# GpSimd adds both halves of a state step to the running sum with one instruction

## What is computed

```python
A_disc = jnp.exp(-jnp.exp(A_log)[None, None] * dt[..., None])
Bx = Bp[:, :, None, :] * dt[..., None] * xs[..., None]
C = Cp @ W_C.T
def step(s, inp):
    A_t, Bx_t = inp
    s = A_t * s + Bx_t
    return (s, s.sum(-1))
...
y = C * ssum + D_param * xs
```

## Time and profile before

| | |
|---|---|
| three runs | 1182.11, 1183.95, 1184.22 us |
| median | 1183.95 us |
| span of the profiled execution | 1183.4 us |
| mean granted TensorE clock | 0.925 of full speed |
| instructions | 15564 |
| HBM traffic | 139.46 MB read, 26.77 MB written |

### The profile page before, as it was taken

The page is one execution under the profiler, slowest core; times in us unless marked ns, Lnnn a source line. Parts: engine busy times, 40 slices in busy tenths (PEclk is TensorE's granted clock), DMA queues, the critical chain, the costliest instruction groups (busy, mean ns, idle before and its releaser), DMA issues.

```text
span 1183.4 us, 15564 instructions
## 1 busy us (share of the span) xinstructions
PE 1028.6 (87%) x4732; PEld 828.0 (70%) x4732; DVE 657.2 (56%) x1148; ACT 642.2 (54%) x1240; POOL 671.5 (57%) x658
## 2 busy tenths in 40 slices
PE   7676497877977878988969899799999999999997
PEld 4323275655656556766757788689999999998886
DVE  7898999899997889877975332001000000110233
ACT  5776778787586786885672433133333333333342
POOL 0755867768589987789695447422433333322221
PEclk9798598888987888999989999899999999999999
DMA  6710100202002016142374582688999988863521
GB/s 195 258 36 1 49 23 19 71 1 89 2 18 72 1 50 218 37 133 80 99 214 141 157 258 59 169 281 245 349 345 310 307 272 275 268 183 63 169 72 54
DMA packets 142244, 166.84 MB, mean 141 GB/s; under 512 B 26424, under 2 KB 127056, under 8 KB 142016
## 3 DMA queue, kind: packets, MB, share of 16 engines
q1 hardware_dynamic: 126480, 147.12, 38.2%
q0 software_dynamic: 15680, 18.72, 8.3%
HBM read 139.46 MB, written 26.77 MB: 140 GB/s over the span
## 4 chain that ended last, share of the span: by engine, by line
PE 45%; POOL 22%; issue 13%; DVE 9%; ACT 6%; SPq 2%; DMA 1%; DVEq 0%; POOLq 0%; ACTq 0%
PE psum L1243 19%; POOL Ssum L1929 10%; PE psum L1210 9%; PE psum L1222 6%; PE psum L1199 6%; POOL list_d L1948 4%; DVE S L1470 3%; ACT A L1771 2%; POOL acc_d L1979 1%; DVE psum L1431 1%; PE psum L1165 1%; POOL gb L1937 1%; POOL scale L1850 1%; PE psum L1186 1%; DMA bb<-b 1%
## 5 line engine op out<-in xcount | busy, mean ns | idle before, releaser
L1929 POOL TENSOR_TENSOR Ssum<-Ssum,S 128x512 f32<-128x512 f32 x217 | 274.3, 1288 | 71.0 <-DVE S L1470 69.9
L1243 PE MATMUL psum<-w,hT 128*128 128x256 f32 x1136 | 255.4, 383 | 7.0 <-issue 5.6
L1243 PEld LDWEIGHTS psum<-w,hT 128*128 128x128 f32 x1136 | 215.7, 192 | 37.5 <-issue 6.7
L1979 POOL DMA_INDIRECT acc_d<-y,ID x71 | 112.8, 1589 | 223.1 <-DMA acc_d<-y,ID 116.5
L1210 PE MATMUL psum<-XT,w 128*128 128x256 f32 x800 | 184.8, 388 | 15.3 <-DMA bb<-b 7.5
L1771 ACT ACTIVATE A<-dts,nea 128x512 f32<-128x512 f32 x245 | 167.6, 717 | 33.9 <-DVE S L1470 27.9
L1210 PEld LDWEIGHTS psum<-XT,w 128*128 128x128 f32 x800 | 153.7, 194 | 43.0 <-issue 12.9
L1431 DVE TENSOR_TENSOR psum<-us,psum 128x512 f32<-128x512 f32 x234 | 149.3, 683 | 34.8 <-PE psum L1116 34.4
L1470 DVE TENSOR_TENSOR_SCAN S<-A,carry,psum 128x512 f32<-128x512 f32 x120 | 148.2, 1264 | 0.0
L1815 ACT ACTIVATE hT<-psum,bb 128x256 f32<-128x256 f32 x200 | 83.4, 472 | 94.9 <-PE psum L1210 94.7
L1595 DVE COPY XT<-psum 128x512 f32<-128x512 f32 x35 | 24.2, 691 | 192.9 <-PE psum L1186 192.8
(11 more groups left out here) (185 smaller groups left out, 1263.9 us busy)
## 6 DMA issues: line engine op xcount, KB each, us to landing
w<-W SPq DMA_DIRECT2D x92, 1024.0 KB, 7.3
bb<-b SPq DMA_DIRECT2D x46, 128.0 KB, 8.1
xnb<-x SPq DMA_DIRECT2D x16, 256.0 KB, 3.0
Xr<-x SPq DMA_DIRECT2D x16, 256.0 KB, 4.4
x_d<-gb SPq DMA_DIRECT2D x8, 512.0 KB, 2.9
xn_d<-nb SPq DMA_DIRECT2D x8, 512.0 KB, 3.1
X<-x_d SPq DMA_DIRECT2D x16, 256.0 KB, 8.7
ACC<-acc_d SPq DMA_DIRECT2D x16, 256.0 KB, 6.3
```

Of the source, the lines that this page charges most:

```text
L1243: t = eng.matmul(bank(g)[:, 256 * k:256 * k + 256], hT[n % 2][:, f, 128 * k:128 * k + 128], w[:, f, :], start=f == 0, stop=f == 7)
L1929: eng.tensor_tensor(to, to, of, ALU.add).then_inc(nsum, 1)
L1979: eng.indirect_dma_start(acc_d, bass.IndirectOffsetOnAxis(ap=ID[:, col, 1:2].bitcast(u32), axis=0), y[n % NY][:, k, :], None, compute_op=A ...
```

## The change

The two tiles of a running sum become one of 128 x 2 x 512, and `S0[i][c]` are views of it. In chunks 1 to 7 GpSimd adds nothing at even k; at odd k one instruction adds two neighbouring slots to both halves. It raises `nsum` by 2. The wait for the scan stays at every k. In chunk 0 nothing changes.

```diff
-        S0 = [[put(f"Ssum{i}{c}", [128, 512]) for c in range(2)] for i in range(2)]
+        Ssum = [put(f"Ssum{i}", [128, 2, 512]) for i in range(2)]
+        S0 = [[Ssum[i][:, c, :] for c in range(2)] for i in range(2)]
...
-                    if n and (i or c and n < EARLY):
-                        to, of = S0[i % 2][c], S[:, s % NS, :]
-                        if i % 2 == 0 and n == 1:
-                            eng.wait_ge(carried, CARRIES * (i // 2) + c + 1)
+                    if i == 0 and c and 0 < n < EARLY:
+                        to, of = S0[0][1], S[:, s % NS, :]
+                        if n == 1:
+                            eng.wait_ge(carried, 2)
                         if n > 1:
                             eng.wait_ge(nsum, added_by_pool(i, k - 2))
                         eng.tensor_tensor(to, to, of, ALU.add).then_inc(nsum, 1)
+                    elif i and c and n:
+                        to, of = Ssum[i % 2], S[:, s % NS - 1:s % NS + 1, :]
+                        if i % 2 == 0 and n == 1:
+                            eng.wait_ge(carried, CARRIES * (i // 2) + 2)
+                        if n > 1:
+                            eng.wait_ge(nsum, added_by_pool(i, k - 2))
+                        eng.tensor_tensor(to, to, of, ALU.add).then_inc(nsum, 2)
```

## The result

| | before | after |
|---|---|---|
| median, 21 runs each | 1182.24 us | 1185.31 us |
| lowest to highest | 1181.14 to 1184.22 | 1182.37 to 1189.68 |
| span of the profiled execution | 1183.4 us | 1181.6 us |

The ratio is 1.0025, 95% interval 1.0018 to 1.0032: the change costs 3.1 us by the medians. In a later measurement, where the kernel before had a median of 1188.01 us, the ratio was 1.0034 (1.0021 to 1.0047). The direction and the range hold; the size was forecast at +5.4 us, and 3.1 came. The spans of the two profiled executions point the other way. The reason is the stretch of transfers and routing between about 700 and 790 us, which differs between executions of one kernel: two traces of the kernel before are together at 710 us, 14.5 us apart at 727 and 3.3 us apart from 784 on.

A forecast was written before the change was run, and what follows sets the result against it. No engine bounds the whole; in the scan stage the path runs through GpSimd's adds and `scale`. Losses of +2.8 and +2.6 us gave +5.4 on 1183.95, so 1189.3 us; 8-in-10 range 1182 to 1193.

The forecast's parts named there:

- The start: The median of three runs of the kernel before, 1183.95 us, to which the forecast adds +5.4 us.
- The duration of a pair: One GpSimd add of 1024 elements: 2.34 us, bounds 1.98 and 2.54; two adds of 512 cost 2.46.
- Term (1): Chunks 2, 3, 5: k = 12's add falls behind the residual, so `scale` comes later; together +2.8 us.
- Term (2): End of chunk 4: VectorE's `ymul` of half 0 waits for the pair k = 30, 31; +2.6 us.
- Term (3): Chunk 1: ScalarE's `nb` stands behind a decay that waited for a scan; costed at nothing, +1.0 us if uncovered.
- Term (4): Chunks 6 and 7: costed at nothing; in chunk 6, +0.9 us without the cover of TensorE's other matmuls.
- Term (5): Rows moving forward (L1012, gathers, scatters between even and odd k) gain up to 1.2 us each; counted as nothing.
- The rival of the lock: Adds hold what VectorE's scans need, longer when twice as long; 56 us over 105 pairs, 1240 us; chance 0.01.
- GpSimd's saving decides: Where GpSimd is behind (339 to 436, 486 to 610 us), 41 pairs save 4.9 us: 1179.0; chance 0.16.
- the loss given back in chunk 6: Sign that the forecast is wrong: chunk 6, where gathers move forward, regains the loss; no size given.

The follow-up runs named there:

- k12_only: Kernel before with only the adds of k = 12 and 13 merged into one instruction; ratio 1.0035 (1.0023 to 1.0047).
- all_late: Kernel before, nothing merged, every even-k add of chunks 1 to 7 put off to odd k; ratio 1.0031 (1.0019 to 1.0043).
- k4_late: Kernel before, nothing merged, only the add of k = 4 put off to k = 5; ratio 0.9974 (0.9962 to 0.9986).
- k4_halves: Kernel before with the add of k = 4 split into two adds of 256 elements; ratio 0.9991 (0.9982 to 1.0).

## Why the prediction was right, and where not

- **The start**: 1189.3 us stands on the median of three runs, 1183.95; with 21 runs it is 1182.24. Of the 4.0 us between 1189.3 and the measured 1185.31, 1.7 come from there, and 2.3 from the sum.
- **The duration of a pair**, 2.34 us: right (median 2.36). The gap between dependent pairs was read from `scale`'s small rows, 0.07 us, and is 0.17. A pair with its gap, 2.53, is therefore at the upper bound of the duration (2.54), and no better than two adds.
- **Term (1), the residual**: the mechanism is right in all three chunks. `scale` came 1.05, 1.21 and 1.04 us later, and VectorE's waits grew by 0.53, 1.16 and 1.06, where 0.97, 0.97 and 0.87 were forecast for both. In chunk 2 the wait grew by less, because VectorE had already lost 0.3 us in waiting for a slot of the ring at 199.0, and got 0.3 back at 223.5. `k12_only` shows that the pair of k = 12 alone is enough for the whole loss, but not that term (1) is: 2.1 of its 3.9 us came in chunk 4, where the prediction had the later `scale` as hidden.
- **Term (2), the end of chunk 4**: the wait grew by 2.69 (2.35 alone, 1.5 in the second trace of the change), and 2.6 was forecast. The first step that failed is that this term was carried into the sum in full. VectorE's 1.2 us of waiting for TensorE's spread at 404.36 was in the trace of before, and 1.3 us of the loss went there; alone, the term left +0.7 us at the last scan and a ratio of 1.0002. The prediction asked what covers a saving, and never what covers a loss.
- **Term (3)**, chunk 1 at nothing: right, the scan of k = 6 in chunk 2 starts within 0.1 us of before in both traces of the change. **Term (4)**, chunk 6 at nothing: VectorE lost 1.04 us (at 531.3) in one trace of the changed kernel and not in the other.
- **Term (5), the gains, "I give them nothing"**: the second step that failed, and the larger one. The prediction asked only which rows the moved adds delay and which come forward. The largest effect of the moved add of k = 4 was on neither, but on a VectorE row that had run beside it: a gain of 2 x 1.1 us, for which the sum has no term.
- **The rival of the lock** had its chance, 0.01, as a loss only, and the prediction closed it with the scans alone. They are not held. But the lock was in the trace of before at two places, and the changed order took it away. Its sign was the other way round: a gain.
- **GpSimd's saving decides**: no. `all_late`, without any saving, has the time of the change. The 22% of POOL in the chain of before, which the prediction held for this rival, has no counterpart in the chain of the changed kernel, which leaves the stage out.
- The mark "the loss given back in chunk 6" was put down as what would make it wrong. Some of it was given back there (1.12 us at 481.0), though by the shift, not by the gathers.

So the direction came out for the reason that was given, and the size did not. With 2.2 us for the shifts and 1.3 for the wait, 5.4 becomes 1.9, between the two traces' last scans (+0.6, with the 1.7 us of chance in it, and +3.3); the medians say 3.1 and 3.5. The range of 1182 to 1193 held because it reached down to no change; 1185.31 lies outside the forecast's own 1186.5 to 1192. The microsecond or two that is left between 1.9 and these is not settled. Why the residual of chunk 4 comes sooner in `k4_late`, and later in the second trace of the change, is open too.

## What to carry to other kernels

When a change moves an instruction of GpSimd, look also at what VectorE runs at its old time and at its new one, and search the trace for small VectorE instructions that last as long as a GpSimd instruction beside them; one tiny row of 1.28 us among rows of 0.17 is such a sign. Merging two instructions makes the first half wait for the second: name each row that stood between them, and keep apart the pairs that stand around a deadline. A loss, like a saving, must be followed to the next wait that was there already, since it costs only what that wait does not take up.

## What the runs showed of the hardware

- A VectorE tensor_scalar or cast of 128 x 8 elements from SBUF to SBUF lasts 0.17 us alone. Begun 0.01 to 0.10 us after a GpSimd tensor_tensor, it lasted 1.28 us beside one of 512 elements, and 0.73 and 0.65 beside two of 256: once for each instruction (`before`, `k4_halves`). No run shows the other order of starting. Scans with a PSUM source beside the same adds are not held (1.18 to 1.22 us).
- GpSimd's tensor_tensor took 0.72 us for 256, 1.27 for 512 and 2.36 for 1024 elements. Adds to different halves of the sum follow each other without idle time (five of 512 in 6.19 us); a pair that waits for the pair before stands idle for 0.17 us first.
- Sixteen like matmuls took 3.72 us in one execution of the changed kernel and 5.41 in another, with a granted clock of 1.00 and 0.93 over the 24 us around them.
